# Latents turned in pairs, L4's small PSUM banks laid out as L3's, and a weight rounding moved one stage ahead

## The reference, cut to what matters

```python
x = x + L0_xattn(ctx, layernorm(x), ...)      # 16 heads, keys and values from ctx
x = x + L0_ffn(layernorm(x), w1, w2)          # linear experts
x = x + L1_xattn(layernorm(x), ctx, ...)      # depooling of patches
x = x + L1_ffn(layernorm(x), ...)             # top-k rows, attention of 16 heads, GELU
x = x + L2_xattn(ctx, layernorm(x), ...)      # 8 heads
x = x + L2_ffn(layernorm(x), w1, conv, w2)    # weights rounded to -1, 0, 1; conv; SiLU
x = x + L3_xattn(ctx, layernorm(x), ...)      # projections, 8 heads
x = x + L3_ffn(layernorm(x), ...)             # latent attention, then 4 experts
```

```python
def mla_attention(x, Wq, Wdkv, Wuk, Wuv, Wo, ln_g, ln_b):   # x is rmsnorm(x, norm1)
    q = heads(x @ Wq.T)                                     # 16 heads of 8
    latent = layernorm(x @ Wdkv.T, ln_g, ln_b)              # 64 numbers a row
    k, v = heads(latent @ Wuk.T), heads(latent @ Wuv.T)
    q, k = rope(q), rope(k)
    scores = where(causal, q @ k.T / sqrt(8), -inf)
    return softmax(scores) @ v  -> rows @ Wo.T

def weight_quant(w):
    scale = 1.0 / clip(mean(abs(w)), 1e-5)
    return clip(round(w * scale), -1, 1) / scale
```

## Time and profile before

| | |
|---|---|
| median of 3 runs | 1465.8 us (1461.6 to 1468.5) |
| the profiled execution's own time | 1465.4 us |
| its span, first to last instruction | 1463.7 us |
| mean granted clock | 0.911 |
| PE busy | 1306.9 us, 89% |
| DVE busy | 932.4 us, 64% |
| ACT busy | 605.9 us, 41% |
| POOL busy | 277.2 us, 19% |
| key loop, first key pass to last | 925.2 to 985.0 us |
| L4's attention, first turn | 987.1 us |

### The profile page before, as it was taken

How to read it: one execution, slowest core, us unless ns; L and a number is a source line. 1 busy time by engine, 2 the same in 40 slices (tenths; PEclk the granted TensorE clock), 3 DMA queues, 4 the chain that set the end, 5 groups by cost and what they waited for, 6 DMA issues and landing times. The chain is left out here.

```text
span 1463.7 us, 37014 instructions
## 1 busy us (share of the span) xinstructions
PE 1306.9 (89%) x13899; PEld 861.5 (59%) x13899; DVE 932.4 (64%) x2810; ACT 605.9 (41%) x1375; POOL 277.2 (19%) x782
## 2 busy tenths in 40 slices
PE   3999988839759979998999997899999969999998
PEld 2888876635447754444657885337888844444443
DVE  4677749975367858996336886325777744454554
ACT  2788845641326642222443556542444421111111
POOL 0122211310313320000002223222454520000000
PEclk9999998958869989997998998656999979999999
DMA  9400000000000000000000000001000000000000
GB/s 288 121 3 3 3 2 2 2 1 1 2 1 2 3 2 1 1 1 1 1 1 2 3 3 1 1 0 59 3 3 3 3 2 0 15 8 7 7 7 15
DMA packets 26390, 21.31 MB, mean 15 GB/s; under 512 B 5936, under 2 KB 22512, under 8 KB 26224
## 3 DMA queue, kind: packets, MB, share of 16 engines
q1 hardware_dynamic: 25216, 18.87, 4.6%
q10 hardware_dynamic: 1008, 0.16, 0.1%
HBM read 16.93 MB, written 2.10 MB: 13 GB/s over the span
## 5 line engine op out<-in xcount | busy, mean ns | idle before, releaser
L703 PE MATMUL ps<-kT,qTm 32*128 32x128 f32 x3200 | 250.9, 291 | 1.2 <-issue 0.6
L671 PE MATMUL ps<-qTm,kT 32*128 32x512 f32 (+1 forms) x1024 | 249.1, 550 | 1.8 <-ACT probs L574 1.4
L703 PEld LDWEIGHTS ps<-kT,qTm 32*128 32x128 f32 x3200 | 226.1, 202 | 6.9 <-issue 4.2
L1933 PE MATMUL ps<-kv_all,ctx_all 128*128 128x512 f32 x256 | 134.1, 605 | 5.8 <-DVE kv_all L1846 5.8
L1870 ACT ACTIVATE kv_all<-ps,b_col 128x512 f32<-128x512 f32 x64 | 44.0, 687 | 216.5 <-PE ps L1911 216.5
L1911 PE MATMUL ps<-q_all,ctx_all 128*128 128x512 f32 x256 | 132.4, 600 | 0.0
L380 DVE TENSOR_REDUCE neg_max<-ps 128x8 f32<-128x1024 f32 x72 | 87.7, 1219 | 67.6 <-PE ps L703 67.3
L574 ACT ACTIVATE probs<-ps 128x1024 f32<-128x1024 f32 x72 | 73.8, 1024 | 119.7 <-PE ps L713 119.7
L860 PE MATMUL ps<-probs,v_wide 128*32 128x128 f32 x3200 | 115.2, 277 | 8.5 <-DVE o_sb L429 3.7
L1846 DVE TENSOR_SCALAR kv_all<-ps,b_col 128x512 f32<-128x512 f32 x64 | 48.0, 750 | 116.4 <-PE ps L1911 116.4
L671 PEld LDWEIGHTS ps<-qTm,kT 32*128 32x128 f32 x1024 | 85.2, 189 | 47.9 <-issue 38.8
(11 more groups left out here) (379 smaller groups left out, 2703.8 us busy)
## 6 DMA issues: line engine op xcount, KB each, us to landing
ctx_all<-in_ctx SPq DMA_DIRECT2D x4, 1024.0 KB, 10.5
x_all<-in_x SPq DMA_DIRECT2D x4, 512.0 KB, 7.1
out<-x_all SPq DMA_DIRECT2D x8, 256.0 KB, 2.3
ctx_all<-in_W1T SPq DMA_DIRECT2D x1, 1024.0 KB, 5.5
tap_w<-in_conv_wT SPq DMA_DIRECT2D x1, 768.0 KB, 6.9
w_l<-in_w SPq DMA_DIRECT2D x2, 256.0 KB, 3.7
above<-in_c_above SPq DMA_DIRECT2D x1, 256.0 KB, 3.4
rope<-in_c_rope SPq DMA_DIRECT2D x1, 256.0 KB, 2.7
```

The source lines that it names most:

```text
L671: nc.tensor.matmul(ps[:, bank, at:at + N], kT[rows_of(g), k, :], qTm[rows_of(g), k, 0:N], start=True, stop=False, skip_group_check=True)
L703: last = nc.tensor.matmul(dst, qTm[rows_of(g), k, 128 * i:128 * i + 128], kT[rows_of(g), k, :], start=False, stop=True, skip_group_check=True)
L1933: nc.tensor.matmul(ps[:, 4 + e % 2, :], w_down[:, c, :], hid[:, c % 4, :], start=c % 4 == 0, stop=c % 4 == 3).then_inc(sem("mo_down"), 1)
```

## The change

1. *Latent pairs.* The key loop runs over 16 pairs. ACT scales the two latents of a pair side by side into the 128 columns of o_sb; one turn gives a tile of 128 partitions, latents of the even item in 0 to 63, of the odd one in 64 to 127; ACT takes it at once (ln_g and ln_b are loaded a second time into partitions 64 to 127). w_h2 becomes [128, 2, 384]: copy i holds the weights in rows 64i to 64i + 63 and zeros elsewhere, so two products over all 128 rows, one per copy, give the keys and values of each item. They go to two neighbouring banks out of 2 to 7, in a rotation of three; the turns use banks 0 and 1. DVE multiplies both items' halves in one instruction (512 elements a partition) in place of four, POOL adds both in one, ACT takes both v in one. w_h2 is cleared by POOL in the prologue and filled by six loads in place of three; with the second copies of ln_g and ln_b that makes five loads more.
2. *L4 in LOW.* The banks, the order in turns() and in DVE's step, and the waits of weighted() become those of L3.
3. *Rounding.* The nine instructions move from the stage behind L1's attention to POOL's end of L1's attention; the clearing of v_wide stays where it was.

```diff
-        LOW = ("L0", "L2") + ("L3",)
+        LOW = ("L0", "L2") + ("L3", "L4")
...
-        w_h2 = sb("w_h2", [64, 384])
+        w_h2 = sb("w_h2", [128, 2, 384])
...
+        pair_halves = probs[:, 0, :].rearrange("p (k i n) -> p k i n", k=RING, i=2)
+        PAIRS = B // 2
+        def pair_banks(p):
+            at = 2 + 2 * (p % 3)
+            return ps[:, at:at + 2, :]
...
-            def key(b, k):
-                dve.wait_ge(sem("la_kv"), b + 1)
-                wait_reuse(dve, after("la_k"), b, RING)
-                half, src = turned_halves[:, k, :], ps[:, 6 + k % 2, :]
-                V.tensor_tensor(half[:, 0:128], src[:, 0:128], rope[:, 2, :], ALU.mult)
-                V.tensor_tensor(half[:, 128:256], src[:, 128:256], rope[:, 3, :], ALU.mult
+            def key(p, k):
+                dve.wait_ge(sem("la_kv"), 2 * p + 2)
+                wait_reuse(dve, after("la_k"), p, RING)
+                wide = rope[:, 2:4, :].rearrange("p r n -> p (r n)").unsqueeze(1).broadcast_to([128, 2, 256])
+                V.tensor_tensor(pair_halves[:, k, :, :], pair_banks(p)[:, :, 0:256], wide, ALU.mult
                                 ).then_inc(sem("la_key_halves"), 1)
...
-                nc.gpsimd.tensor_tensor(kv_all[:, b, 0:128], half[:, 0:128], half[:, 128:256],
+                nc.gpsimd.tensor_tensor(kv_all[:, 2 * p:2 * p + 2, 0:128], half[:, :, 0:128], half[:, :, 128:256],
                                         ALU.add).then_inc(sem("la_k"), 1)
...
+            def scale(p, k):
+                wait_reuse(act, after("la_latent_turned"), p, 2)
+                for b in (2 * p, 2 * p + 1):
+                    at = LATENT * (b % 2)
+                    nc.scalar.activation(o_sb[:, k % 2, at:at + LATENT], lat_raw[:, b, :], ACT.Identity,
+                                         bias=lat_shift[:, b:b + 1], scale=lat_scale[:, b:b + 1]
+                                         ).then_inc(sem("la_latent"), 1)
...
+            def take_v(p, k):
+                act.wait_ge(sem("la_key_halves"), p + 1)
+                nc.scalar.activation(kv_all[:, 2 * p:2 * p + 2, 128:256], pair_banks(p)[:, :, 256:384],
                                      ACT.Copy).then_inc(sem("la_v"), 1)
-            steps(act, B, [(0, scale), (1, take_turned), (3, take_v)])
+            steps(act, PAIRS, [(0, scale), (1, take_turned), (3, take_v)])
...
-            def keys(b, k):
-                pe.wait_ge(sem("la_latentT"), b + 1)
-                wait_reuse(pe, after("la_v"), b, 2)
-                nc.tensor.matmul(ps[:, 6 + k % 2, 0:384], oT[0:LATENT, k % 2, :], w_h2[:], start=True,
-                                 stop=True).then_inc(sem("la_kv"), 1)
-            steps(pe, B, [(1, turn_latent), (2, keys)])
+            def keys(p, k):
+                pe.wait_ge(sem("la_latentT"), p + 1)
+                wait_reuse(pe, after("la_v"), p, 3)
+                for i in range(2):
+                    nc.tensor.matmul(pair_banks(p)[:, i, 0:384], oT[:, k % 2, :], w_h2[:, i, :], start=True,
+                                     stop=True).then_inc(sem("la_kv"), 1)
+            steps(pe, PAIRS, [(1, turn_latents), (2, keys)])
...
+        ] + [(w_h2[64 * i:64 * i + 64, i, 128 * c:128 * c + 128], t_in[w])
+             for i in range(2) for c, w in enumerate(("WukT", "WukT_turned", "WuvT"))
+        ] + [(col(n)[64:128, :], t_in[n].rearrange("(s one) -> s one", one=1)) for n in ("ln_g", "ln_b")
...
+            nc.gpsimd.memset(w_h2[:], 0.0).then_inc(sem("w_h2_cleared"), 1)
...
-                 gpsimd=lambda e: attention_gpsimd(e, "L1", TILES, 16, False),
+                 gpsimd=lambda e: (attention_gpsimd(e, "L1", TILES, 16, False), round_weights(e)),
...
-            dict(vector=expand_vector, scalar=expand_scalar, tensor=expand_tensor, gpsimd=expand_aside),
+            dict(vector=expand_vector, scalar=expand_scalar, tensor=expand_tensor, gpsimd=lambda e: pads_gpsimd(e, 8)),
```

41 lines of the change are left out of this document (15 added, 26 removed).

## The result

The changed kernel takes **1425.0 us** (median of 4 runs, 1422.0 to 1427.7) against 1466.2 (4 runs, 1461.6 to 1468.5) on the same chip: a ratio of 0.9722, 95% interval 0.9688 to 0.9757. The forecast was 1426.0, its range 1418 to 1436. The profiled execution took 1422.6 (span 1420.8), 42.9 less in span than the one before.

What follows compares the result with a forecast made beforehand. The prediction took PE to bound the latent key loop, held at 1.2 GHz by products over 64 rows, and also L4. From the profiled 1465.4, 1465.4 - 34.3 - 4.5 - 0.3 = 1426.3 us, range 1418 to 1436.

Steps and rivals of the forecast that it cites:

- Part 1: Key loop: pairing latents over 128 rows raises the clock, so L4 begins at 952.8 instead of 987.07, -34.3 us.
- the rise 5 us behind it: Key loop: the clock rises to 2.4 GHz 5 us after the first key pass, between the 3 and 11 seen.
- the pair of 1.43: Key loop: a pair's 1664 columns take 1.43 us at 2.4 GHz, by the query loop's rate.
- the tail of 1.8: End of key loop: 1.8 us from PE's last pass to L4's first turn, 1.2 before.
- The rule of the Trainium skill quoted in the prediction: TensorE: the clock gate opens by how busy PE has been, with no word on rows.
- L4's start, put at 0: Key loop to L4: the clock falls again in the pause and L4's start costs what it did, 0 us.
- The rival's price for a warm start: L4's start: the clock does not fall because the pause is shorter, -6 us, total 1420; chance 0.22.
- Part 2: L4's steps: weighted sums no longer wait for o_sb, 0.16 us an item over 28 items, -4.5 us, bounds 0 and -6.1.
- What was feared as late next: L4's step: L671 or L436 ends the wait at the same place, nothing from part 2, total 1431; chance 0.13.
- Part 3: Weight rounding fits under L1's attention tail on POOL; the next stage loses a few DVE waits, -0.3 us, bounds 0 and -1.
- I take 0, since POOL is late for nobody: L1's attention tail: DVE adds and POOL's moved work side by side cost 0 us, though +4 at most was possible.
- The rival's mechanism: L1's attention tail: DVE's two-SBUF-input adds and POOL exclude each other, +4 us, total 1430; chance 0.04.

Runs made afterwards that it cites:

- e4: The kernel before, item by item, with the key product widened to 128 rows, the lower 64 of weights and latents zeros; 1438.7 us.
- e6: The changed kernel with both products of a pair over the same 64 rows (0 to 63), leaving part of the computation out; 1456.1 us.
- e5: The changed kernel with each of a pair's two products reading only its own 64 rows, no zeros multiplied; 1422.6 us.
- e12: e7 plus one more unread 128-row filler product on PE in each of L4's next three steps; 1418.1 us.
- e7: The changed kernel plus unread PE filler products: 9 ahead of the keys, 3 behind them, 1 in L4's first step; 1419.1 us.
- e2: The kernel before with only L4's small banks set as in L3 (L4 in LOW); 1458.7 us.
- e3: The kernel before with only the weight rounding moved behind L1's attention on POOL; 1468.7 us.
- e8: The changed kernel with POOL's three two-SBUF-operand products put back into the expansion stage, the six roundings left beside L1's attention; 1430.7 us.
- e10: The changed kernel with the weight rounding back in the expansion stage, but only once DVE's normalised rows are done; 1424.2 us.

## Why the prediction was right, and where it was not

**Part 1, mechanism and size right.** The first pass was put at 925.6 and stood at 924.9; the rise 5 us behind it came after 4.4; the pair of 1.43 was 1.40; the tail of 1.8 was 1.7. The last pass ended at 949.5 and not 951.0, so the stage gained 35.2 and not 34.3. That rows free the clock was taken from three places in the trace that all spoke for it; e4 and e6 show it for this loop, and e5 corrects it: rows at work together, in one product or in two. The rule of the Trainium skill quoted in the prediction (TensorE: Matmul & The Clock Gate, "What's actually happening") would have given no change in e4 and a risen clock in e6; both measurements (0.50 to 1.00 in e4; 0.50 in e6 with PE busy for 4.00 of 4.00 us) go against it in that form, which knows busyness alone.

**L4's start, put at 0.** The clock did fall, as taken. The step failed in its tacit second half, that the low stretch behind the fall has a fixed length: it was 17 us here, 25 before, and anything from 17 to 33 in the other runs. The rival's price for a warm start, 6, fits the one execution that had it: 169.0 to 163.4 in e12, filler included. Its reason, that the pause is short, is not enough: in e7 the pause was filled and the clock fell 7 us into L4.

**Part 2, mechanism right, term too small.** The wait for o_sb is gone (0.50 to 0.32 between L713 and L860). The term was 0.16 a step with an upper bound of 0.19; it is 0.24. Of the missing 0.08, 0.02 are the wait itself (0.50 - 0.32 = 0.18), and 0.06 are in the half step that I did not look at: with the picks ahead of the turns, L722 follows L776 by 0.15 (before, the picks stood between them), and L671 follows L783 by 1.54 and not 1.60. What was feared as late next was not: L671 stands 1.35 behind L860 as before. 6.2 us in e2, not 4.5.

**Part 3, wrong.** "I take 0, since POOL is late for nobody" is the step that failed. Two of the three adds take 1.42 us where 0.34 is usual, each until about 0.15 behind the end of the product of POOL beside it, and 1.5 us of that reach the end of L1; the next stage gives back 0.9. The rival's mechanism happened, at 1.5 of its 4 us: all three products fell beside the adds of a single step. The rule cited beside it (SBUF — State Buffer, "SBUF: two separate sides": a DVE instruction with two SBUF inputs and a GpSimd one that reads SBUF exclude each other for the whole instruction) agrees with POOL's products: e3 has the long adds, e8 and e10 without products there have short ones. It does not agree with the roundings, which read SBUF as well: in e8 the adds ended 0.64 us ahead of the rounding beside them.

**The sum** was 3.7 above the profiled execution: 0.9 of it are part 1, 2.8 are L4 (1.7 the size of part 2, 1.1 its start); the stages ahead of the keys gave 0.6 where part 3 had 0.3, and 0.3 came back behind L4. Part 3's own +0.6 cannot be seen in that 0.6: in the execution after, L1's end came 4 us earlier than before, with other falls and rises of the clock, and most of that was lost again in L2's first steps. That the median, 1425.0, came within 1.3 us of the forecast is partly luck: the same kernel measured 1421.1 on another chip, both inside the range, and the terms missed by up to 1.7 us each.

## What to carry to other kernels

Read the granted clock by stage before counting instructions: a dense loop of half-height products can sit at 1.2 GHz for its whole length, and filling the array's rows, with a second item or even with zeros (28 us in e4), can be worth more than any instruction saved. Work moved to an idle engine is not free because nobody waits for its result; look at which instructions of DVE and GpSimd keep each other waiting while it runs. A term for a steady loop must be read over the whole period, both halves of a step, and a term smaller than what the clock's own falls and rises shift (here 5 us) has to be judged in the stage, not by the total.
